# Attention of layers 2 and 3: ScalarE's queue fills the stacks of the first two queries

## The reference

```python
q = _split_heads(query @ Wq.T + bq)      # query = layernorm(x)
k = _split_heads(key @ Wk.T + bk)        # key = value = ctx_1024
v = _split_heads(value @ Wv.T + bv)
scores = jnp.einsum('bhqd,bhkd->bhqk', q, k) / np.sqrt(DK)
scores = jnp.where(mask[:, None, :, :] == 0, -1e9, scores)
p_attn = jax.nn.softmax(scores, axis=-1)
x = jnp.einsum('bhqk,bhkd->bhqd', p_attn, v)
```

## Time and profile before

| | us |
|---|---|
| median of 3 runs (lowest, highest) | 2356.03 (2353.68, 2358.13) |
| the profiled execution's own time | 2350.17 |
| its span, which all times of rows refer to | 2348.4 |
| PE busy | 1961.3 (84% of the span) |
| DVE busy | 1256.7 (54%) |
| ACT busy | 921.5 (39%) |
| POOL busy | 776.6 (33%) |
| time in which 16 DMA engines worked for q1 / q10 / q0 | 27.6% / 0.8% / 8.5% |

### The profile page before, as it was taken

The page is one execution under the profiler, slowest core; times in us unless marked ns, Lnnn a source line. Parts: engine busy times, 40 slices in busy tenths (PEclk is TensorE's granted clock), DMA queues, the critical chain, the costliest instruction groups (busy, mean ns, idle before and its releaser), DMA issues. The chain is left out here.

```text
span 2348.4 us, 41459 instructions
## 1 busy us (share of the span) xinstructions
PE 1961.3 (84%) x13179; PEld 1585.9 (68%) x13201; DVE 1256.7 (54%) x4235; ACT 921.5 (39%) x2196; POOL 776.6 (33%) x1055
## 2 busy tenths in 40 slices
PE   6849999987899999999849988995693897797594
PEld 5637766665799889989649975653582675454583
DVE  2542225633788888888420017984435445785423
ACT  3723321423233333333423334763442344675320
POOL 1012211110444444454211124420454646542132
PEclk9959999988899999999969999996796998999697
DMA  4232221000501110110069954436467475533294
GB/s 145 102 121 62 62 83 43 16 19 24 63 19 33 33 30 18 33 28 2 8 231 346 341 183 113 111 75 252 155 150 250 136 144 137 115 93 117 81 346 141
DMA packets 173308, 261.88 MB, mean 112 GB/s; under 512 B 23088, under 2 KB 138800, under 8 KB 169008
## 3 DMA queue, kind: packets, MB, share of 16 engines
q1 hardware_dynamic: 152176, 209.30, 27.6%
q0 software_dynamic: 16704, 45.64, 8.5%
q10 hardware_dynamic: 4224, 4.33, 0.8%
HBM read 181.19 MB, written 37.75 MB: 93 GB/s over the span
## 5 line engine op out<-in xcount | busy, mean ns | idle before, releaser
L2222 PE MATMUL heads_ps_c<-heads_band,heads_sT 128*128 128x129 f32 x3072 | 369.2, 277 | 13.9 <-DVE heads_band L2447 12.8
L2222 PEld LDWEIGHTS heads_ps_c<-heads_band,heads_sT 128*128 128x128 f32 x3072 | 355.3, 192 | 24.1 <-issue 22.2
L508 POOL DMA_INDIRECT weights_xg<-xn_rows,token_of x197 | 191.3, 971 | 443.1 <-DVE token_of L698 171.2
L2385 POOL TENSOR_SCALAR heads_band<-heads_shifts,heads_taps 128x130 f32<-128x130 f32 x384 | 253.0, 673 | 242.5 <-PE heads_ps_c L2222 238.8
L2315 ACT ACTIVATE heads_probs<-heads_mixes,heads_least 128x256 f32<-128x256 f32 x256 | 116.1, 500 | 343.9 <-DVE heads_least L2460 343.9
L2447 DVE SCALAR_TENSOR_TENSOR heads_band<-heads_shifts,heads_taps,heads_band 128x130 f32<-128x130 f32 x768 | 226.8, 351 | 18.6 <-POOL heads_band L2385 13.9
L1893 ACT ACTIVATE heads_probsT<-heads_ps_e 128x512 f32<-128x512 f32 x256 | 148.2, 597 | 69.1 <-PE heads_ps_e L1736 61.1
L1047 PE MATMUL experts_ps_g<-weights_w,experts_xT 128*128 x504 | 136.6, 395 | 10.2 <-issue 6.9
L1070 PE MATMUL experts_ps_y<-weights_w,experts_hT 128*128 (+1 forms) x486 | 133.7, 384 | 1.4 <-DVE experts_y L1132 1.1
L1712 PE MATMUL heads_ps_m<-heads_stackK,heads_stackQ 96*128 96x256 bf16 x512 | 100.8, 282 | 31.2 <-DMA heads_stackQ<-heads_q_pieces 12.4
L1104 ACT ACTIVATE experts_silu<-experts_ps_g 128x128 f32<-128x128 f32 (+1 forms) x165 | 53.2, 322 | 153.8 <-PE experts_ps_u L1052 81.0
(11 more groups left out here) (425 smaller groups left out, 4189.2 us busy)
## 6 DMA issues: line engine op xcount, KB each, us to landing
experts_w<-in_experts_dram SPq DMA_DIRECT2D x23, 2180.0 KB
weights_w<-in_experts_dram SPq DMA_DIRECT2D x16, 1536.0 KB
weights_w<-in_experts_dram SPq DMA_DIRECT2D x32, 768.0 KB
y_rows<-experts_y SPq DMA_DIRECT2D x125, 128.0 KB
heads_stackK<-heads_k_pieces SPq DMA_DIRECT2D x192, 64.0 KB, 2.6
heads_stackQ<-heads_q_pieces SPq DMA_DIRECT2D x192, 64.0 KB, 2.5
weights_w<-in_experts_dram SPq DMA_DIRECT2D x8, 1088.0 KB
xn_rows<-xn SPq DMA_DIRECT2D x4, 2048.0 KB, 7.5
```

What stands on the lines that cost most here:

```text
L508: pool.indirect_dma_start(self.xg[:, u, :], None, xn_dram, bass.IndirectOffsetOnAxis(ap=tb.token_of[:, j:j + 1], axis=0)).then_inc(self.x_ ...
L2222: last = pe.matmul(out[:, qc * SEQ + k0:qc * SEQ + k1], sT[:, h % 2, kc, qc * P + dq:qc * P + dq + P], band[:, h % 2, dq, w0:w0 + k1 - k0] ...
L2385: last = pool.tensor_scalar(band[:, h % 2, dq, :], shifts[:, 0, :], taps[:, r % 2, h, dq * TAPS:dq * TAPS + 1], None, ALU.mult)
```

## The change

`fill_queries(0)` and `fill_queries(1)` leave SP's order. ACT gets a function of the same name, with the same wait and the same six DMAs, and calls it behind `take_query(2)` for query 0 and behind `take_query(3)` for query 1. No DMA and no wait is added or dropped: 12 DMAs in each of the two stages go through q10 in place of q1.

```diff
             context(6)
-            fill_queries(0)
-            fill_queries(1)
             context(7)
             fill_keys(2)
             fill_queries(2)
...
+            def fill_queries(u):
+                act.wait_ge(q_ready, u + 1)
+                for n, (a, _) in enumerate(PRODUCTS):
+                    act.dma_start(stackQ[n * HD:(n + 1) * HD, u % SLOTS, :, :], q_pieces[:, u % SLOTS, a, :])\
+                        .then_inc(q_stacked[u % SLOTS], 16)
+
...
             take_query(2)
+            fill_queries(0)
             take_query(3)
+            fill_queries(1)
             arriving.deviation(act, 2)
             pair_rows(2)
```

## The result

| | us |
|---|---|
| before, median of 18 runs beside the changed ones (lowest, highest) | 2356.90 (2352.49, 2360.34) |
| changed, median of 18 runs (lowest, highest) | 2361.86 (2355.52, 2368.45) |
| ratio, with its 95% interval | 1.0023 (1.0014 to 1.0031) |
| span of the profiled execution, before and changed | 2348.4 and 2356.0 |

A forecast was written before the change was run, and what follows sets the result against it. PE was taken as the busiest engine, its scores in both openings started by the landing of query 0's fills. Layer 2 +5.6, clock 0 and layer 3 0 gave +5.6 us: 2356.03 to 2361.6 us, range 2357.5 to 2366.

The forecast's parts named there:

- Issue and landing in layer 2: Layer 2's opening: query 0's sixth fill issued 3.6 us later and landing slower beside SP's fills; first score +5.6 us.
- Rival 1: Queues hardly disturb each other in layer 2: layer 2 costs 3.6 to 4.6, whole +2.5 to +4.6 us; chance 0.34.
- Rival 2: Contention as in layer 1 in both layers: layer 2 +6.3 to +8.4, layer 3 +1.6, whole +8 to +11; chance 0.12.
- Rival 4: The move matters nowhere, as keys or masks hold the first score; chance 0.08 together with rival 3.
- Behind the issues on ACT: Layer 2: second take, query 1's fills and deviation(2) come later on ACT, hidden by the late first score; zero.
- Layer 2, clock: PE's longer idle time may slow the projection behind it to half clock; zero, between -0.5 and +1.3 us.
- Layer 3: Layer 3's opening: sixth fill issued 2.3 us later but landing in 3.6 us with fewer transfers in flight; 0.
- Rival 3: Layer 3's opening gives back up to 5.4 us through an earlier context of batch 7; sum -1.8; 0.08 with rival 4.

The follow-up runs named there:

- e2: The changed kernel with the change in layer 3 only, layer 2 as before; ratio to the kernel before 1.0001 (0.9991 to 1.0011).
- e3: The changed kernel, but SP waits behind the context of batch 7 until query 0 has landed before filling keys of round 2; ratio to before 0.9999.
- e8: e3 once more, the same kernel; ratio to the kernel before 1.0009 (0.9992 to 1.0026).
- e6: The changed kernel with query 0's fills back on SP behind the context of batch 6, only query 1's on ACT; ratio to before 1.0005.
- e1: The changed kernel with the change in layer 2 only, layer 3 as before; ratio to the kernel before 1.0013 (1.0004 to 1.0022).
- e10: The kernel before, with POOL's gathers of pairs 4 and 5 in layer 3 held until the context of batch 7 has landed; ratio 0.9996.
- e4: The kernel before, all fills on SP, but SP waits until the third query is taken before issuing query 0's fills; ratio 1.0003.
- e7: The changed kernel once more, unchanged; ratio to the kernel before 1.0019 (1.0005 to 1.0033).
- e11: Kernel before, query 0's fills ahead of batch 6's context; layer 3's gathers (pairs 4, 5) and fills from round 3's keys await query 1's row maxima; ratio 1.0002.

## Why the prediction was right, and where it wasn't

| step | forecast | profile of the changed kernel |
|---|---|---|
| first issue by ACT | 1417.7 | 1417.48 |
| sixth starts | 1420.95 | about 1420.7 |
| first score, layer 2 | 1425.5 | 1425.73 (+5.59 from the stage's start) |
| deviation(2), does DVE wait? | 1425.6, no | 1425.36, no (in use at 1429.24) |
| opening behind the first score | 27.6 | 25.18 |
| first score, layer 3 | within 1 us | -0.21 |
| end of layer 3 | 0 | +2.37; not settled (e2) |
| time | +5.6 | +5.4 (+3.3 to +7.3) |

The mechanism was right: a later landing of query 0 in layer 2 holds the scores, and the scores hold the kernel. That the time came within 0.2 us is luck. The interval is 4 us wide, and two terms taken as zero were not, or may not have been: the opening gave some of layer 2's 5.6 us back, and layer 3 may have cost 1 to 2.

*Issue and landing in layer 2* came as forecast. The division of its 5.6 us into 3.6 for the issue and 2.0 for the landing holds within a microsecond: e3 and e8 give 2.8 and 3.1 for the issue with the keys held, and 2.75 and 1.95 for the neighbours. Rival 1 would have had SP's fills undisturbing: they weren't (34.6 against 31.8). Rival 2 fails on the first scores: 5.6 us later in layer 2, not 6.3 to 8.4, and no later in layer 3, where it had +1.6. Rival 4, that the move matters nowhere, fails by 6.53 us of idle time.

The Trainium skill (DMA: Bandwidth & Descriptors, section Issuing engines are not separate DMA queues) had the queues interleave on the same engines, which e3 bears out, and the issue usually small beside the DMA, which doesn't fit six in a row: they take 3.86 us, and the last lands 2.5 us behind its issue where it is undisturbed (e3).

*Behind the issues on ACT* zero was right for the reason given, and e6 shows the other half, with a smaller size: 0.74 us where I had written some 3 for a first score at its old time. In e6 deviation(2) comes 31.9 us from the stage's start and not at the 34.7 that I had worked with, since ACT issues six DMAs ahead of it and not twelve.

*Layer 2, clock* is the step that failed. The text put it at "zero, between -0.5 and +1.3", and called the forecast wrong if the opening behind the first score shrinks. It shrank by 2.4 us, in e1 too (25.21), and by 1.8 against the mean of three unchanged openings. I had looked for what a longer idle time costs the projection just behind it, and that cost is there: the key projection of batch 5 takes 2.95 us. But a value projection (3.04 to 1.89) and a query projection (2.04 to 1.10) further on, slow before, no longer were. They stand at full and nearly full clock in the unchanged e10 too (1.89 and 1.24), so how much of this the shift does is open. Over three profiles of each kind the first score is 5.6 us later and the end 4.7, so the term was about -1 on the whole, in place of 0; single profiles scatter by more than that (201.5 to 203.1 unchanged, 205.3 to 208.0 changed).

*Layer 3* at 0 holds for its first score. Its stage ends 1.4 to 3.2 us later in the three changed profiles than in the two unchanged ones, and e2's ratio allows up to 2.6.

*Rival 3* named the wait of 4.27 us as the one to look at in the second half of layer 3's opening, but misread its cause: it has the context land some 9 us behind its issue, where the packets took 2.2, and the row itself names DVE as the releaser. With that context secured (e10) the same stall comes, 5.5 us long, and the opening gains 0.8.

*Not settled.* The profiles have e3, e8 and e4 lengthen layer 2 by 3.6, 1.6 and 3.8 us against the one profile of before, while their ratios are 0.9999, 1.0009 and 1.0003. Two profiles of one kernel differ in the same stage by 2.3 us (changed, e7) and 2.0 (e3, e8), so one profile prices a stage no finer than that; the timed ratios say that those three versions lose less than 0.3%. No version here is shown to beat the kernel before.

## What to carry to other kernels

Move a DMA to another engine's queue only if that engine reaches the issue no later than the old one did: here the data was ready at 1412.7, ACT at 1417.5, and a second queue doesn't win those 5 us back. Then look at what the old queue does with the time it is given: it issued the next fills, which nobody needed for some 30 us, into the same DMA engines. And when a wait is removed from an opening, ask what caused it and where that cause goes: in e11 a stall went with its gathers into the loop, and of nearly 8 us of shorter opening 2.1 were left at the stage's end and none in the time.

## What the runs showed of the hardware that was not expected

- A DMA share over 1.2 is a queue, not throughput: with one queue busy (e3, 1419 to 1424) windows of 1 us moved 76 to 123 GB/s at 0.32 to 0.53, with two (changed kernel, 1420 to 1426) 107 to 123 at 1.21 to 1.27.
- A burst of eight indirect gathers, issued over some 10 us, goes with a stall of VectorE of 3.8 to 7.4 us, which ends 1.8 to 2.4 us behind the last of their issues in twelve of fourteen profiles. In seven of them ScalarE's wait for TensorE ends at the same moment; the results of TensorE come late, and the trace doesn't say why.
- The stretches of half clock don't stand at fixed instructions: two projections of layer 2 take 3.04 and 2.04 us in the kernel before, 1.89 and 1.10 in the changed one, and 1.89 and 1.24 in e10, where layer 2 is that of before.
